# Twelve-layer perceiver block on one core: the first batch's context is asked for one stage ahead in three cross-attentions

## The reference

```
x = x + f(layernorm(x))
```

```
q  = x @ Wq.T + bq;  k, v = split(context @ Wkv.T + bkv)
out = softmax(q k.T / 4) v;   y = out @ Wo.T + bo
```

```
q, k, v = x @ Wq, context @ Wk, context @ Wv
out = softmax(q k.T / 8) v;   y = out @ Wo + bo
```

## Time and profile before

| | us |
|---|---|
| median of 3 runs | 2962.85 |
| lowest, highest run | 2956.24, 2963.18 |
| the profiled execution | 2951.73 |
| its span | 2949.9 |
| mean granted clock of PE | 0.97 |

### The profile page before, as it was taken

One profiled execution on the slowest core, in us unless ns is written; L12 is line 12 of the kernel. 1 busy time (PEld: TensorE's weight loads), 2 busy tenths in 40 slices (PEclk: granted clock), 3 DMA queues, 4 the chain that ended last, 5 costly groups with the idle time before them and its releaser, 6 DMA issues. The chain is left out here.

```text
span 2949.9 us, 46309 instructions
## 1 busy us (share of the span) xinstructions
PE 2742.8 (93%) x18078; PEld 1924.7 (65%) x18078; DVE 1463.0 (50%) x2504; ACT 990.6 (34%) x2207; POOL 150.8 (5%) x302
## 2 busy tenths in 40 slices
PE   8889978999998989799999988879999999999899
PEld 4667964666666569456666768737676664667545
DVE  4573234777777430344544461345454443899500
ACT  2332225666665213322222111222222224666200
POOL 1002021001000010100000010200000000000000
PEclk9989999999999989899999989999999999999999
DMA  9235852111111039321111025421111110222100
GB/s 301 90 128 175 301 193 67 44 30 44 30 30 47 1 112 329 104 71 65 65 48 60 33 109 213 165 69 65 63 46 65 54 38 1 72 72 73 39 1 14
DMA packets 96791, 259.99 MB, mean 88 GB/s; under 512 B 18916, under 2 KB 44232, under 8 KB 89048
## 3 DMA queue, kind: packets, MB, share of 16 engines
q1 hardware_dynamic: 85512, 240.17, 24.3%
q0 software_dynamic: 3840, 10.49, 1.1%
q10 hardware_dynamic: 7248, 6.65, 0.7%
HBM read 236.13 MB, written 21.14 MB: 87 GB/s over the span
## 5 line engine op out<-in xcount | busy, mean ns | idle before, releaser
L2200 DVE TENSOR_REDUCE buf<-acc 128x1 f32<-128x1024 f32 x128 | 150.7, 1219 | 367.8 <-PE acc L2094 367.8
L2169 ACT ACTIVATE buf<-acc,buf 128x1024 f32<-128x1024 f32 x128 | 142.5, 1113 | 365.7 <-DVE buf L2200 365.7
L2088 PE MATMUL acc<-buf 128*128 128x512 f32 x512 | 241.0, 614 | 21.5 <-DMA buf<-in_ctxT 18.1
L357 PE MATMUL acc<-buf 128*128 128x256 f32 (+4 forms) x768 | 225.6, 488 | 11.2 <-PEq L87 11.2
L2114 PE MATMUL acc<-buf 128*128 128x256 f32 x1024 | 231.7, 379 | 1.5 <-ACT buf L2179 1.5
L2114 PEld LDWEIGHTS acc<-buf 128*128 128x128 f32 x1024 | 190.7, 190 | 25.7 <-issue 1.9
L357 PEld LDWEIGHTS acc<-buf 128*128 128x128 f32 (+2 forms) x768 | 132.3, 191 | 106.5 <-issue 98.8
L2216 DVE COPY buf<-acc 128x1024 f32<-128x1024 f32 x128 | 156.0, 1219 | 91.7 <-PE acc L2103 91.7
L2545 ACT ACTIVATE buf<-acc,buf 128x512 f32<-128x512 f32 x256 | 172.4, 685 | 75.1 <-DVE buf L2579 75.0
L2579 DVE TENSOR_REDUCE buf<-acc 128x1 f32<-128x512 f32 x256 | 158.9, 682 | 76.6 <-PE acc L2457 76.6
L2088 PEld LDWEIGHTS acc<-buf 128*128 128x128 f32 x512 | 94.2, 194 | 127.6 <-issue 102.7
(11 more groups left out here) (395 smaller groups left out, 4408.4 us busy)
## 6 DMA issues: line engine op xcount, KB each, us to landing
buf<-in_L_ffn_W SPq DMA_DIRECT2D x52, 1024.0 KB, 6.5
buf<-in_ctx SPq DMA_DIRECT2D x48, 768.0 KB, 4.5
buf<-in_ctxT SPq DMA_DIRECT2D x64, 512.0 KB, 5.6
buf<-in_L_ffn_w SPq DMA_DIRECT2D x36, 704.0 KB
buf<-state_rows SPq DMA_DIRECT2D x32, 512.0 KB
buf<-in_ctxT SPq DMA_DIRECT2D x96, 128.0 KB, 5.6
buf<-in_L_ffn_w SPq DMA_DIRECT2D x18, 640.0 KB
buf<-in_ctxT SPq DMA_DIRECT2D x32, 256.0 KB
```

The source lines that it names most:

```text
L357: ins = pe.matmul(banks[n % nbanks][rows(r), 0:w], lhsT, rhs, start=(k == 0), stop=(k == len(pairs) - 1))
L2088: pe.matmul(acc_s[y][:, halves(h)], q0[:, b, 2 * r:2 * r + 2, :], ct0[x][:, halves(h)], start=True, stop=False)
L2169: act.activation(probs[u % 4][:, :], acc_s[u % 2][:, :], ACT.Exp, bias=negmax[:, u % 4:u % 4 + 1], accum_out=total[:, u % 4:u % 4 + 1]).th ...
L2200: dve.tensor_reduce(negmax[:, u % 4:u % 4 + 1], acc_s[u % 2][:, :], AX.X, ALU.max, negate=True).then_inc(max_ready, 1)
```

## The change

The buffers of batch 0 (keys, and for 8 heads the context) are taken from the attention stage and given to the layer around it, so that they exist in the stage in front. The second buffer of each pair stays in the attention stage; the total is the same there and larger in the front stage. SP issues batch 0's transfers in the front stage: in L1_xattn in `normed_jobs` behind the nine weight loads, in L2_xattn and L3_xattn in `matmul_jobs`, where SP has nothing else to issue. They count on two semaphores of their own that are never cleared, so PE waits for a running total. In the attention stage SP's loop begins with batch 1, and PE's first wait is on the new semaphore. No instruction of an engine that computes is added, removed or moved, and the transfers are the same in number and size.

```diff
@@ class Chip
+        self.first_keys_in, self.first_context_in = nc.alloc_semaphore("first_keys_in"), nc.alloc_semaphore("first_context_in")
+        self.first_keys = self.first_contexts = 0
@@ attend_eight(chip, X, q0, q1, Wv0, Wv1, Wo, bias, first, w, ident, ahead)
-        ctx = [st.sbuf(P, KT, CC) for _ in range(2)]
-        ct0, ct1 = [st.sbuf(P, SK) for _ in range(2)], [st.sbuf(P, HALF) for _ in range(2)]
+        ct0, ct1, ctx = [first[0], st.sbuf(P, SK)], [first[1], st.sbuf(P, HALF)], [first[2], st.sbuf(P, KT, CC)]
...
-            for b in range(B):
+            for b in range(1, B):
...
-                if p % 2 == 0:
-                    pe.wait_ge(keys_in[x], 48 * (b // 2) + 48)
+                if p == 0:
+                    pe.wait_ge(chip.first_keys_in, 16 * chip.first_keys)
+                elif p % 2 == 0:
+                    pe.wait_ge(keys_in[x], 48 * ((b - 1) // 2) + 48)
...
-                if y == 0:
-                    pe.wait_ge(ctx_in[x], 16 * (p // 4) + 16)
+                if p == 0:
+                    pe.wait_ge(chip.first_context_in, 16 * chip.first_contexts)
+                elif y == 0:
+                    pe.wait_ge(ctx_in[x], 16 * ((p // 2 - 1) // 2) + 16)
@@ eight_head_xattn
+        ct0, ct1, ctx = sb(P, SK), sb(P, HALF), sb(P, KT, CC)
+
+        def first_batch(sync):
+            sync.dma_start(ct0[:, :], w["ctxT"][0, 0:P]).then_inc(chip.first_keys_in, 16)
+            for h in range(2):
+                sync.dma_start(ct1[h * C1:h * C1 + C1, :], w["ctxT"][0, P:CC, halves(h)]).then_inc(chip.first_keys_in, 16)
+            sync.dma_start(ctx[:, :, :], w["ctx"][0]).then_inc(chip.first_context_in, 16)
+            chip.first_keys += 3
+            chip.first_contexts += 1
...
-            matmul_jobs(chip, jobs, [])
-        attend_eight(chip, X, q0, q1, Wv0, Wv1, Wo, bias, w, ident, ahead)
+            matmul_jobs(chip, jobs, [], also=first_batch)
+        attend_eight(chip, X, q0, q1, Wv0, Wv1, Wo, bias, (ct0, ct1, ctx), w, ident, ahead)
@@ sixteen_head_xattn
+        first_ct0, first_ct1 = sb(P, SK), sb(P, SK)
+
+        def first_batch(sync):
+            sync.dma_start(first_ct0[:, :], w["ctxT"][0, 0:P]).then_inc(chip.first_keys_in, 16)
+            for g in range(2):
+                sync.dma_start(first_ct1[g * C1:g * C1 + C1, :], w["ctxT"][0, P:CC]).then_inc(chip.first_keys_in, 16)
+            chip.first_keys += 3
...
-                           (bk[:, :], w["bk"]), (bv[:, :], w["bv"])], setup=shifts,
+                           (bk[:, :], w["bk"]), (bv[:, :], w["bv"])], setup=shifts, also=first_batch,
...
-            ct0, ct1 = ([st.sbuf(P, SK) for _ in range(2)] for _ in range(2))
+            ct0, ct1 = [first_ct0, st.sbuf(P, SK)], [first_ct1, st.sbuf(P, SK)]
...
-                for b in range(B):
+                for b in range(1, B):
...
-                    if j == 0:
-                        pe.wait_ge(ctx_in[x], 48 * (n // 2 // PER_BATCH // 2) + 48)
+                    if n == 0:
+                        pe.wait_ge(chip.first_keys_in, 16 * chip.first_keys)
+                    elif j == 0:
+                        pe.wait_ge(ctx_in[x], 48 * ((n // 2 // PER_BATCH - 1) // 2) + 48)
```

More of the change, by code:

```diff
@@ L2024, in _, with attend_eight @@
             chip.wait_far(sync)
-def attend_eight(chip, X, q0, q1, Wv0, Wv1, Wo, bias, w, ident, ahead):
+def attend_eight(chip, X, q0, q1, Wv0, Wv1, Wo, bias, first, w, ident, ahead):
     nc = chip.nc
```

## The result

| | before | after |
|---|---|---|
| median of 4 runs, us | 2960.99 | 2927.93 |
| lowest, highest | 2956.24, 2963.18 | 2926.02, 2930.32 |
| ratio, 95% interval | | 0.9890 (0.9877 to 0.9903) |
| the profiled execution, us | 2951.73 | 2928.09 |

The change takes 33.1 us off the median (28.7 to 36.4 by the interval). 2928.1 was predicted, against 2927.93 measured. The code has moved down by some lines in the changed kernel (L2088 is L2092, L2094 is L2098, L2436 is L2461, L2394 is L2417, L357 is L359).

A forecast was written before the change was run, and what follows sets the result against it. The kernel was taken as a chain of PE work in stages (PE busy 2742.8 of 2949.9 us). Terms 10.0 + 3.0 + 6.2 + 2.8 + 9.7 + 3.0 = 34.7 us off 2962.85 gave 2928.1, range 2915 to 2943.

The forecast's parts named there:

- 1: L1_xattn's wait: PE starts at 447.55 instead of 457.58, 10.0 us gained, with keys landing just in time.
- 3: L2_xattn's wait: PE begins with POOL at 1250.75 instead of 1256.97, 6.2 us gained.
- 5: L3_xattn's wait and clock: PE starts at 1943.2 instead of 1952.89, 9.7 us, and first matmuls gain 3.0 us.
- 2: L1_xattn's clock: the four projections run at full clock after a shorter rest, 3.0 us gained, bounds 0 and 3.0.
- 4: L2_xattn's clock: the first eight matmuls run at step 1's pace, 2.8 us gained.
- rival b: L1_xattn's keys land late, at 8.3 us, and its clock falls too: gain 30.4 us, time 2932.4; chance 0.10.
- 6: Front stages: three more transfers in L1's, four in the others, cost nothing; L357's 64 matmuls still take 14.00 us.
- 7: Attention stages: batch 1's keys, issued when batch 0's were, arrive in time, so the whole gain reaches the end.
- (c): The seam waits go but PE waits for batch 1's keys instead, giving the gain back: about 2956 us; chance 0.03.
- (d): Whole kernel: PE rests less and its granted clock falls throughout, slower at 2983 us; chance 0.02.
- Rival (a): The three seams: the clock falls despite short rests, leaving a gain of 25.9 us, time 2936.9; chance 0.12.
- The sign that was to go with it: Whole profile: attention stages otherwise as long as before, so the changed kernel's span is 2915.2 us.

The follow-up runs named there:

- order-only run: The kernel before, with batch 0's keys and context issued in the attention stage itself but ahead of the far loads; 0.9978 of before.
- Zeros in the waits: The kernel before, transfers unmoved, PE multiplying zeros while waiting for batch 0's keys; 1.0029 of before with 38, 24, 38 products, 0.9967 with 19, 12, 20.
- the pause: The changed kernel, with PE waiting for POOL's bias add before its first matmul in the three attention stages; 0.9959 of before.
- second profile of before: The kernel before, profiled again with no edit; 2959.73 us.
- the parts: The kernel before with only the 16-head edits (L1_xattn), 0.9956 of before, or only the 8-head edits (L2_xattn and L3_xattn), 0.9924.

## Why the prediction was right

**The reading of the seams (1, 3, 5).** Right to a tenth of a microsecond against the profile that it was read from. PE starts with POOL and not 10.06, 6.23 and 9.67 us behind it; 10.0, 6.2 and 9.7 were forecast. The order-only run shows that an earlier place on the queue would not have done it.

**The clock (2, 4, 5).** L1's projections took 11.94 us (from 14.97), L2_xattn's eight matmuls 3.60 (from 6.44), L3's 3.61 (from 6.64): 3.0, 2.8 and 3.0 as forecast. Zeros in the waits gave back the same terms alone, and the pause took 1.6, 2.8 and 2.7 us of them away again, with 5.65 us of rest and more. The mechanism is right. The sizes hold for the one profile that they were read from: at the same seams the second profile of before has 1.9, 1.8 and 2.4 us, and the profiles of the parts, at the seams that they leave alone, 1.6 (L1), 1.9 (L2) and 1.9 (L3). So the three terms are 1.6 to 3.0 us each, by the execution, and the first profile had the largest of every one.

**Batch 0's keys in L1 (1, rival b).** Landed 5.6 us after issue, where I took 6.3; in time by 1.4 us in this profile. Rival (b) did not come.

**What hides the rest (6, 7).** The front stages kept their 14.00 us, no wait for batch 1 came, and everything behind moved up: the parts multiply to the whole. So (c) is out. (d) is out: PE's mean granted clock went from 0.970 to 0.974 (0.968 to 0.972 in the second profiles).

**Rival (a) and the freely running watch.** The rule of the Trainium skill (TensorE: Matmul & The Clock Gate, "What's actually happening"), that the watch on PE's activity is not aligned with the kernel, gave a sum between 25.9 and 34.7. At the changed kernel's own seams it did not show: in each of its profiles their clock stayed up, so rival (a) did not come. At the seams of before it did, in the price (6.44 and 5.43 us for the same eight matmuls), and in the neighbourhood too. The same rest of 1.84 us in L1_xattn's first step cost the clock in six of the thirteen profiles that have it, and not in the others. By the Trainium skill (TensorE: Matmul & The Clock Gate, "What's actually happening") that is what one must expect of a watch that runs freely; here, with the fall at the end of the stage, it is worth 0 to 3 us. All this may be the 1.6 us between 34.7 forecast and 33.1 measured. Over the three profiles that have each seam as it was, the rests mean 9.9, 6.6 and 9.4 us and the clock's terms 2.2, 2.2 and 2.4, together about 33. That is an estimate from a few profiles; the difference is not settled, and it lies well inside 0.3%.

**The time.** That 2928.1 met 2927.93 to 0.2 us is luck. The base of 2962.85 was 1.9 us above the median of the four runs, the gain of 34.7 was 1.6 above the measured one, and the two cancel. 2962.85 - 34.7 = 2928.1 leaned on the median of three runs, not on the profiled execution; the profile's own 2951.73 would have given 2917.0. The sign that was to go with it, a span of 2915.2, did not come. It was 2926.3, although the stages lost 34.9 us: 7.6 us of the difference stand up to L1_xattn, 1.1 between L2 and L3 and 2.6 behind L3. The second profile of before and the first of after show why the median was the right base: the larger part of the profile's lead over it lay in a stretch that has nothing to do with the change.

## What to carry to other kernels

Where a stage begins with a wait for its own first load, price the wait and the clock that PE loses in it: here 26 us of waiting cost 9 more in one profile, and 25 us cost 6 more in another. So read a clock's price from more than one profile. Ask for that load as far ahead as a stage with a quiet queue, and only for the piece that the first instruction reads. When two profiles disagree with the medians, cut both at marks that the change does not move, and compare piece by piece. A mark behind several instructions of a queue brings in their own time, as the fourth load did here.

## What the runs showed of the hardware

- The same rest of 1.84 us, in the same instructions, sometimes costs the clock and sometimes not, and a fall costs about 1.6 us there (10.33 against 8.68 us). After rests of 5.65 us and more at the seams it always fell, which cost 1.6 to 3.0 us each time; after 1.1 and 1.85 us there it never did.
- The same holds of a longer rest. Behind 3.96 us, at the 64 matmuls of L357 in a late front stage, it stayed up in two of the fourteen profiles (14.05 us, before and order only) and fell in twelve (15.74 to 16.68 us).
- Zero matrices keep the clock up: 12 products of zeros in L2_xattn's wait did, although 1.23 us of rest remained behind them.
- With one program, the layers up to L1_xattn took 447.5 us in one execution and 456.2 in another. In the last set of runs all four kernels took 224 to 226 us between L2_xattn and L3_xattn where the others took 234 to 238, and before itself took 2946.7 in that set, against 2961.3 and 2956.1 in the two sets before it. Each of these sets ran on another chip; the cause was not looked for, and it is why every ratio is against the kernel before of the same set.
